# One masked add and one maximum for four heads, and the router's top two moved beside its logits

## The chip, the cores and the metric

One core of a Trainium2 chip runs the whole program in one launch. The metric is the device time in microseconds (us), from launch to end, the median over runs. Everything else of the chip is idle.

## The reference, cut to what matters

x and ctx are 32 batches of 128 rows by 512. One layer of cross attention with 32 heads of 16 columns, then a mixture of 8 experts of which each row takes two.

```python
x = x + xattn(layernorm(x), mask, ctx, Wq, Wk, Wv, Wo, gate)
x = x + moe(layernorm(x), router_w, w1, w2)

# xattn: keys and values of the rows themselves, with a mask, and those of ctx ("adapter"), without
scores = einsum('bhqd,bhkd->bhqk', rope(q), rope(k)) / 4 + mask      # mask is [32, 1, 128, 128]
w = softmax(scores)
attn = w @ v + tanh(gate) * softmax(einsum('bhqd,bhkd->bhqk', rope(q), a_k) / 4) @ a_v
out = attn @ Wo

# moe
logits = x @ router_w.T
topk_vals, topk_idx = top_k(logits, 2)
topk_w = softmax(topk_vals)
# rows sorted by expert, two ragged matmuls with silu(gate) * up between them, weighted and summed
```

## The kernel before, in words

The program has two phases. `attention_phase` (L88) computes attention and the router, batch by batch, and writes for every expert a list of its rows to HBM; `expert_phase` (L1195) walks 71 tiles of 128 list entries. The change touches the first alone.

Each engine has its own instruction stream, written out by hand, and they meet only through semaphores; an `Event` counts one kind of step, and `at(n)` is the count at which batch n has done it. `walk` (L219) gives every engine the same outline: `first`, then one `step` for each batch b, then `last`. Batches 0 to 3 and the last two are written out, the 26 between them run in a loop of 13 iterations of two batches each. A step works on several batches at once: attention proper (exponentials, values) of b; projections, rotation, stacking, scores and maxima of n = b + 1; layer norm of m = b + 2; output projection, second norm and router logits of d = b - 1; the router's choice, counts and lists of c = b - 2.

TensorE's step (L1127) sets the frame. It goes through u = 0 to 15, two for each of eight groups of four heads (own keys and adapter keys). For each u it does `scores_T(b, u)`, which recomputes scores transposed with mask and minus maximum in PSUM, then extra work by u, and `values(b, u - 1)`. The extra work: u = 1 the q projection of n; u = 2 its k projection, `ctx_turn` and `out_turn(d)`; u = 3 `places(c)` (L1121), two small matmuls over the one-hot sum `sel` that count the rows of each expert; u = 4 `out_project(d)`; u = 5 `ak(n)`; u = 7 `h_turn(d)`; u = 8 `router(d)` (its logits go to md[1]); from u = 8 on `stack(n, u - 8)`, and from u = 9 on `scores(n, u - 9)` (L1042). `scores` fills the PSUM banks md[1] (adapter keys) and md[0] (own keys) with a group's scores. Each has a single buffer: the four matmuls into md[1] wait for `s_ad` of the group before, the four into md[0] for `s_own`. After u = 15 come the two value projections and `x_turn(m)`, then `max_turn(n)`.

VectorE's `maxima(n, g)` (L704) reads the two banks: one reduce over md[1] (L707), then for each of four heads a fused instruction that adds the mask to the head's scores in md[0] and keeps the maximum (L710). In the profile each of these is two records, CUSTOM_DVE_ANT_0 and DVE_READ_ACCUMULATOR2_ANT. `neg_max` (L714) turns the maxima of all groups into three bf16 parts; `max_turn` on TensorE and a copy (L731) end the chain, and L731 marks where the next batch's `scores_T` may begin.

The rest of VectorE's step (L855) is in this order: `norm_out(d)`, `sum_out(d)`, `ctx_lo(n)`, `mask_lo(n)`, `out_low(d)`, `rotate_q(n)` (L685, L689), `router_top(c)` (L792), `router_counts(c)`, `rotate_k(n)`, `router_weights(c)`, `values_out(b, 0)`, `residual(d)`, `norm_h(d)`, `h_low(d)`, `ak_low(n)`, `values_out(b, 1)`, `router_logits(d)` (L788), `stats_x(m)`, `maxima(n, 0)`, `norm_x(m)`, `maxima(n, 1)`, `maxima(n, 2)`, `values_out(b, 2)`, maxima 3 to 6, `values_out(b, 3)`, `maxima(n, 7)`, `neg_max(n)`. Here n, m, d and c are left out where there is no such batch: the step of batch 1 has a d and no c.

`router_top` takes the eight logits `lg` of a row, finds the two highest (L796), their gap (L798), and turns each into a one-hot row by way of its lowest index (L802 to L814), then adds the two (`sel`, L818). It is a chain of some 14 instructions over 8 columns, each waiting for the one before. `router_counts` waits for `f_p`, the end of `places`.

GpSimd (POOL) rotates and subtracts for the low halves, and at the end of each step `enter_lists(c)` issues eight indirect DMAs (L425), one for each expert; it does so behind `x_low(m)`, which follows `stats_x` and `norm_x` on VectorE and `x_high(m)` on ScalarE (at u = 11). ScalarE does the exponentials (L528), the copies out of PSUM (`out_T` L543, `stack_out` L513) and the high halves.

Of the kernel before, what the change touches and what calls it, by code (L numbers as in the profile page):

```python
# [21 lines left out]
ALU, ACT, AX = mybir.AluOpType, mybir.ActivationFunctionType, mybir.AxisListType  # L22

P = 128
# [13 lines left out]
GROUPS = NH // 4  # L38
# [49 lines left out]
def attention_phase(nc, ctx, dram, keep):  # L88

    def sb(name, shape, dt):  # L90
        return ctx.enter_context(nc.sbuf_tensor(name, shape, dt))
# [4 lines left out]
    def ev(name, per=1):  # L96
        return Event(keep["semaphores"].enter_context(nc.semaphore(name)), per)
# [23 lines left out]
    msk = sb("msk", [P, 2, P], F32)  # L121
# [17 lines left out]
    mx = sb("mx", [P, 2, NH], F32)  # L139
# [35 lines left out]
    sm = [bank[:, :].rearrange("p (a n) -> p a n", a=4) for bank in md]  # L175
# [22 lines left out]
    w_sc, w_hi, w_lo = ev("w_sc"), ev("w_hi"), ev("w_lo")  # L198

    stk_t, stk_o = ev("stk_t", GROUPS), ev("stk_o", GROUPS)  # L200
    s_pe, s_ad, s_own = ev("s_pe", GROUPS), ev("s_ad", GROUPS), ev("s_own", GROUPS)
    m_part, mp3, mp_t, m_T = ev("m_part", 4), ev("mp3"), ev("mp_t"), ev("m_T")

# [419 lines left out]
    def _(dve):  # L623
# [80 lines left out]
        def maxima(n, g):  # L704
            dve.wait_ge(s_pe.sem, s_pe.at(n, g + 1))
            dve.wait_ge(s_own.sem, s_own.at(n, g))
            dve.tensor_reduce(mx[:, 1, 4 * g:4 * g + 4], sm[1][:, :, :], AX.X, ALU.max).then_inc(s_ad.sem, 1)  # L707
            for j in range(4):
                h = 4 * g + j
                i = dve.tensor_tensor_reduce(sm[0][:, j, :], sm[0][:, j, :], msk[:, n.par, :], 1.0, -3.4028235e38,  # L710
                                             ALU.add, ALU.max, mx[:, 0, h:h + 1])
            i.then_inc(s_own.sem, 1)

        def neg_max(n):  # L714

# [23 lines left out]
        def norm_out(n):  # L739

            dve.wait_ge(av_s.sem, av_s.at(n))
            dve.reciprocal(rc[:, :, :], avs[:, :, :, HD]).then_inc(n_rc.sem, 1)  # L742
            dve.wait_ge(n_rc.sem, n_rc.at(n))
            dve.tensor_tensor(rc[:, :, 1], rc[:, :, 1], tg[:, :], ALU.mult).then_inc(n_rg.sem, 1)
            dve.wait_ge(n_rg.sem, n_rg.at(n))
            dve.tensor_tensor(avs[:, :, 1, 0:HD], avs[:, :, 1, 0:HD],
                              rc[:, :, 1:2].to_broadcast([P, NH, HD]), ALU.mult).then_inc(n_o2.sem, 1)

        def sum_out(n, x_batch):
            if x_batch:  # L750
                dve.wait_ge(x_hi.sem, x_hi.at(x_batch))
                dve.wait_ge(x_lo.sem, x_lo.at(x_batch))
            dve.wait_ge(n_o1.sem, n_o1.at(n))
            dve.wait_ge(n_o2.sem, n_o2.at(n))
            dve.wait_ge(h_hi.sem, h_hi.at(n.shift(-1)))
            dve.wait_ge(h_lo.sem, h_lo.at(n.shift(-1)))
            dve.tensor_tensor(heads(nat), avs[:, :, 0, 0:HD], avs[:, :, 1, 0:HD], ALU.add).then_inc(n_o.sem, 1)
# [30 lines left out]
        def router_logits(n):  # L788
            dve.wait_ge(r_p.sem, r_p.at(n))
            dve.tensor_copy(lg[:, :], md[1][:, 0:NE]).then_inc(r_lg.sem, 1)  # L790
# [64 lines left out]
        def step(b, c, d, n, m):  # L855
            if d:
                norm_out(d)
                sum_out(d, n)
            if n:
                ctx_lo(n)  # L860
                mask_lo(n)
            if d:
                out_low(d)
            if n:
                rotate_q(n)
            if c:
                router_top(c)
                router_counts(c)
            if n:
                rotate_k(n)  # L870
            if c:
                router_weights(c)
            values_out(b, 0)
            if d:
                residual(d)
                norm_h(d)
                h_low(d)
            if n:
                ak_low(n)
            values_out(b, 1)  # L880
            if d:
                router_logits(d)
            if m:
                stats_x(m)
            if n:
                maxima(n, 0)
            if m:
                norm_x(m)
            if n:
                maxima(n, 1)  # L890
                maxima(n, 2)
            values_out(b, 2)
            if n:
                for g in range(3, 7):
                    maxima(n, g)
            values_out(b, 3)
            if n:
                maxima(n, 7)
                neg_max(n)
# [12 lines left out]
        def last(n):  # L912
            norm_out(n)
            sum_out(n, None)
            router_top(n.shift(-1))
            out_low(n)
            router_counts(n.shift(-1))
            router_weights(n.shift(-1))
            residual(n)
            norm_h(n)  # L920
            h_low(n)
            router_logits(n)
            router_top(n)
            router_counts(n)
            router_weights(n)
            experts_slots()

        def experts_slots():
# [37 lines left out]
            assert made[0] == TAB  # L966

        walk(dve, step, first, last)


# [575 lines left out]
```

## Time and profile before

| | us |
|---|---|
| runs | 2768.54, 2767.58, 2760.34; median 2767.58 |
| profiled execution, its own time | 2786.29 |
| its span, first to last instruction | 2784.5 |
| granted clock over the span | 0.830 |
| attention phase, up to the last router work | until about 2283 |
| expert phase | about 501 |
| busy: TensorE, VectorE, ScalarE, GpSimd | 2405.2, 1409.8, 1178.9, 946.0 |

Busy times are sums over the span; a busy TensorE is not a fast one, since the clock it is granted moves between two levels, 1.2 and 2.4 GHz, which the profile shows as 0.50 and 1.00. The line PEclk shows the mean in tenths in 40 slices of 69.6 us, so a slice is about one batch. The chain that ended last is followed back only through the expert phase; for the attention phase waits and timelines must be read. A releaser "remote" means that the wait ended with a semaphore's update that no instruction record explains at that time.

### The profile page before, as it was taken

To read this page: it belongs to the slowest core of one execution; us is meant where nothing else is said; L and a number is where in the kernel's file an instruction comes from. 1 tells how busy PE (TensorE), PEld (TensorE's weight loads), DVE (VectorE), ACT (ScalarE), POOL (GpSimd) and SP (SyncE) were. 2 spreads that over 40 slices of the span, in tenths; PEclk is the share of its full clock that TensorE was granted. 3 is DMA by queue.
4 is the path that set the end of the run, shared out by engine and by line. 5 is a ranking of instruction groups with operands and counts; after the bars stand their busy time and mean duration, and the time that the engine had idled before them with its cause. 6 is when DMAs were issued, how large, how long until landed. Compare 5 with 4: busy or idle time off the path is not lost. (4 is left out here: it accounts for less than half of the span.)

```text
span 2784.5 us, 55409 instructions
## 1 busy us (share of the span) xinstructions
PE 2405.2 (86%) x18441; PEld 1746.0 (63%) x18442; DVE 1409.8 (51%) x4993; ACT 1178.9 (42%) x2100; POOL 946.0 (34%) x948
## 2 busy tenths in 40 slices
PE   4999898889888979898888888888888836999997
PEld 2777666667666756576666666666666624666664
DVE  4466555556555645555555555555555433333332
ACT  3554444444444434344444444444444304444443
POOL 2223333333333333333333333333333223444443
PEclk7898887788788878787878787888788858999999
DMA  2010000000000000010000000000000204444444
GB/s 88 15 38 28 22 23 23 22 23 22 23 22 23 22 13 27 11 32 17 27 16 27 18 25 21 22 23 22 23 22 19 44 14 106 83 83 83 83 83 68
DMA packets 65264, 98.06 MB, mean 35 GB/s; under 512 B 24512, under 2 KB 28608, under 8 KB 64512
## 3 DMA queue, kind: packets, MB, share of 16 engines
q0 software_dynamic: 24096, 37.51, 7.7%
q1 hardware_dynamic: 40928, 57.30, 6.8%
q8 instruction: 156, 2.56, 0.4%
q14 instruction: 84, 0.69, 0.1%
HBM read 59.12 MB, written 35.65 MB: 34 GB/s over the span
## 5 line engine op out<-in xcount | busy, mean ns | idle before, releaser
L1097 PE MATMUL av<-vv,pr 128*128 128x17 f32 x4096 | 636.5, 292 | 6.2 <-ACT pr L528 6.2
L1097 PEld LDWEIGHTS av<-vv,pr 128*128 128x128 f32 x4096 | 628.6, 233 | 20.2 <-ACT pr L528 6.8
L528 ACT ACTIVATE pr<-st 128x512 f32<-128x512 f32 x512 | 305.0, 596 | 587.0 <-PE st L1083 408.6
L707 DVE TENSOR_REDUCE mx<-md 128x4 f32<-128x512 f32 x256 | 176.7, 690 | 340.4 <-remote 214.4
L1051 PE MATMUL md<-kk,qz 128*128 128x128 f16 x2048 | 214.9, 255 | 136.1 <-DVE mx L707 74.7
L1415 PE MATMUL y<-w1s,hgT 128*128 x1704 | 279.2, 314 | 4.4 <-ACT hgT L1329 4.4
L425 POOL DMA_INDIRECT lists<-row,posi x256 | 249.6, 975 | 85.4 <-issue 85.4
L710 DVE CUSTOM_DVE_ANT_0 md<-md,msk 128x128 f32<-128x128 f32 x1024 | 265.0, 321 | 0.0
L1051 PEld LDWEIGHTS md<-kk,qz 128*128 128x128 f16 x2048 | 157.4, 115 | 167.8 <-issue 112.3
L411 POOL TENSOR_TENSOR avs<-avs,rc 128x512 f32<-128x512 f32 x32 | 34.6, 1082 | 662.8 <-DVE rc L742 662.8
L1074 PE MATMUL st<-qz,kk 128*128 128x256 f16 x1024 | 213.8, 293 | 27.8 <-issue 20.1
L520 ACT ACTIVATE qz<-ma 64x256 f16<-64x256 f16 x512 | 191.6, 374 | 104.4 <-remote 86.7
L1083 PE MATMUL st<-mT,hsel 96*128 96x128 bf16 x2048 | 225.7, 238 | 1.1 <-issue 1.1
L1415 PEld LDWEIGHTS y<-w1s,hgT 128*128 128x128 f16 x1704 | 164.2, 98 | 95.8 <-issue 4.9
L737 DVE COPY avs<-av 128x272 f32<-128x272 f32 x128 | 56.5, 441 | 313.9 <-PE av L1097 278.0
L1083 PEld LDWEIGHTS st<-mT,hsel 96*128 96x128 bf16 x2048 | 153.3, 107 | 94.9 <-issue 84.7
L1078 PE MATMUL st<-identr,mskp 128*128 128x512 f32 x512 | 209.5, 495 | 0.0
L522 ACT ACTIVATE kk<-ma 128x512 f16<-128x512 f16 x256 | 152.9, 597 | 3.0
L1434 PE MATMUL y<-w2s,yT 128*128 (+1 forms) x639 | 150.3, 379 | 0.9 <-DVE yT L1393 0.9
L982 PE MATMUL ma<-w_v,xT 128*128 128x512 f16 x384 | 146.5, 559 | 0.0
L710 DVE DVE_READ_ACCUMULATOR2_ANT mx<- 128x1 f32 x1024 | 145.0, 142 | 0.0
L1329 ACT ACTIVATE hgT<-px 128x1024 f16<-128x1024 f16 x71 | 72.7, 1024 | 156.7 <-PE px L1405 156.7
(200 smaller groups left out, 3968.7 us busy)
## 6 DMA issues: line engine op xcount, KB each, us to landing
wst<-in_w SPq DMA_DIRECT2D x32, 352.0 KB, 3.3
cin<-in_ctx SPq DMA_DIRECT2D x32, 256.0 KB, 3.5
xin<-in_x SPq DMA_DIRECT2D x32, 256.0 KB, 3.7
out<-x SPq DMA_DIRECT2D x32, 256.0 KB, 2.0
h_pairs<-ohs SPq DMA_DIRECT2D x32, 256.0 KB
lists<-row,posi POOLq DMA_INDIRECT x256
msk<-in_mask SPq DMA_DIRECT2D x32, 64.0 KB, 3.1
lrow<-lists SPq DMA_DIRECT2D x71, 1.0 KB, 3.6
```

The source lines that it names most:

```text
L425: pool.indirect_dma_start(out=dram["lists"], out_offset=bass.IndirectOffsetOnAxis(ap=posi[:, e:e + 1], axis=0), in_=row[:, e, :], in_offse ...
L520: act.activation(qz[r, pairs, j, :], bank[r, 0:2], ACT.Copy)
L522: act.activation(kk[:, :, pairs, :], keys, ACT.Copy).then_inc(stk_o.sem, 1)
L528: act.activation(pr[:, path, :, :], st[path][:, :, :], ACT.Exp).then_inc(p_ex.sem, 1)
L707: dve.tensor_reduce(mx[:, 1, 4 * g:4 * g + 4], sm[1][:, :, :], AX.X, ALU.max).then_inc(s_ad.sem, 1)
L710: i = dve.tensor_tensor_reduce(sm[0][:, j, :], sm[0][:, j, :], msk[:, n.par, :], 1.0, -3.4028235e38, ALU.add, ALU.max, mx[:, 0, h:h + 1])
L1051: i = pe.matmul(sm[path][:, j, :], qz[:, h // 2, h % 2, :], keys[:, h // 2, :], start=True, stop=True)
L1074: pe.matmul(bank[:, 2 * j:2 * j + 2, :], keys[:, p, :], qz[:, p, :, :], start=(j == 0), stop=False, skip_group_check=True)
L1078: pe.matmul(bank[:, :, :], mskp[:, n.par, part, :], identr[:, :].unsqueeze(1).to_broadcast([P, 4, P]), start=False, stop=False, skip_group ...
L1083: i = pe.matmul(bank[:, j, :], hsel[:, h:h + 1].to_broadcast([3 * NH, P]), mT[:, path, :], start=False, stop=(j == 3), skip_group_check=True)
L1097: i = pe.matmul(av[g // 2 % 2][:, h % 8, path, :], pr[:, path, j, :], vv[:, n.par, path, h, :], start=True, stop=True)
L1415: i = pe.matmul(y1[s.par][j][:, 0:F], hgT[:, s.par, a, c, :], w, start=(n == 0), stop=(n == 11))
```

## The change

In `maxima`, the four fused instructions of a group become one `tensor_tensor` that adds the mask (broadcast over the four heads) to all of md[0] in place, and one `tensor_reduce` over it. A new event `s_mask` makes the reduce wait for the add. `router_top(c)` leaves the head of VectorE's step; `router_top(d)` now stands right behind `router_logits(d)`, one step earlier for the same batch. In `last`, the call for the batch before the last is gone, since its step has done it.

```diff
@@ attention_phase
     stk_t, stk_o = ev("stk_t", GROUPS), ev("stk_o", GROUPS)
+    s_mask = ev("s_mask", GROUPS)
@@ maxima(n, g)
             dve.tensor_reduce(mx[:, 1, 4 * g:4 * g + 4], sm[1][:, :, :], AX.X, ALU.max).then_inc(s_ad.sem, 1)
-            for j in range(4):
-                h = 4 * g + j
-                i = dve.tensor_tensor_reduce(sm[0][:, j, :], sm[0][:, j, :], msk[:, n.par, :], 1.0, -3.4028235e38,
-                                             ALU.add, ALU.max, mx[:, 0, h:h + 1])
-            i.then_inc(s_own.sem, 1)
+            dve.tensor_tensor(sm[0][:, :, :], sm[0][:, :, :], msk[:, n.par, :].unsqueeze(1).to_broadcast([P, 4, P]),
+                              ALU.add).then_inc(s_mask.sem, 1)
+            dve.wait_ge(s_mask.sem, s_mask.at(n, g + 1))
+            dve.tensor_reduce(mx[:, 0, 4 * g:4 * g + 4], sm[0][:, :, :], AX.X, ALU.max).then_inc(s_own.sem, 1)
@@ step(b, c, d, n, m) of VectorE
             if c:
-                router_top(c)
                 router_counts(c)
@@
             if d:
                 router_logits(d)
+                router_top(d)
             if m:
                 stats_x(m)
@@ last(n) of VectorE
             norm_out(n)
             sum_out(n, None)
-            router_top(n.shift(-1))
             out_low(n)
             router_counts(n.shift(-1))
```

## Rows read from the trace of the kernel before

**Rows 1.** The page, part 2: granted TensorE clock in 40 slices of the span.
```profile
PEclk7898887788788878787878787888788858999999
```
**Rows 2.** Windows of whole batches: stretch, length, busy by engine, clock, DMA share, GB/s.
```profile
core 0: us, PE busy (x) PEld busy (x) DVE busy (x) ACT busy (x) POOL busy (x), PEclk, DMA share, GB/s
126.10:177.70 51.60, 49.53 (x470) 37.96 (x470) 31.71 (x110) 30.01 (x57) 14.53 (x11) 1.00 0.09 30
...
1989.60:2061.20 71.60, 61.87 (x472) 46.04 (x472) 39.10 (x137) 30.29 (x58) 22.48 (x20) 0.79 0.07 22
2061.20:2129.60 68.40, 61.39 (x472) 46.00 (x472) 38.95 (x138) 30.57 (x58) 22.49 (x20) 0.80 0.06 19
```
**Rows 3.** Windows within these batches: the stretches at the lower clock.
```profile
2074.60:2081.40 6.80, 6.48 (x25) 3.97 (x26) 4.43 (x19) 1.64 (x3) 2.40 (x2) 0.50 0.00 0
...
2105.30:2125.80 20.50, 18.03 (x96) 14.00 (x97) 8.13 (x42) 5.15 (x12) 4.49 (x5) 0.50 0.01 1
...
2002.90:2013.10 10.20, 7.38 (x32) 4.46 (x31) 7.37 (x24) 4.55 (x7) 4.80 (x3) 0.50 0.00 1
```
**Rows 4.** Waits over the span: total us, times, longest us.
```profile
PE md L1124 <- DVE sel L818: 88.6, 31, 6.0
...
PE md L1051 <- DVE mx L707: 74.7, 52, 4.3
...
PE md L1051 <- DVE mx L710: 20.2, 50, 0.5
```
**Rows 5.** Timeline, VectorE at group 0 and TensorE at group 1.
```profile
2094.84 0.69 DVE L707 TENSOR_REDUCE mx<-md 128x4 f32<-128x512 f32 x1
2095.45 0.29 DVE L710 CUSTOM_DVE_ANT_0 md<-md,msk 128x128 f32<-128x128 f32 x1
...
2096.40 0.54 DVE L650 TENSOR_SCALAR nat<-xin,mv 128x512 f32<-128x512 f32 x1
...
2096.47 0.61 PE L1051 MATMUL md<-kk,qz 128*128 128x128 f16 x8
```
**Rows 6.** Groups of VectorE's instructions: busy us, mean ns, idle before them.
```profile
L710 DVE CUSTOM_DVE_ANT_0 md<-md,msk 128x128 f32<-128x128 f32 x1024 | 265.0, 321 | 0.0
...
L710 DVE DVE_READ_ACCUMULATOR2_ANT mx<- 128x1 f32 x1024 | 145.0, 142 | 0.0
...
L746 DVE TENSOR_TENSOR avs<-avs,rc 128x512 f32<-128x512 f32 x32 | 46.6, 1455 | 1.1
...
L685 DVE TENSOR_TENSOR t<-ma,rope 128x512 f32<-128x512 f32 x64 | 43.8, 685 | 15.5 <-POOL qs L379 14.5 <-PE ma L982 1.0
```
**Rows 7.** Timeline, opening pass: the last of seven such rows, 2.40 us apart.
```profile
62.73 0.69 DVE L707 TENSOR_REDUCE mx<-md 128x4 f32<-128x512 f32 x1 [0.70 <-PE md L1051]
```
**Rows 8.** Timeline of TensorE around `places` in the batch from 2061.2.
```profile
2070.76 1.02 PE L1097 MATMUL av<-vv,pr 128*128 128x17 f32 x8
...
2074.92 0.19 PE L1124 MATMUL md<-sel,tri 128*128 128x8 bf16 x1 [2.69 <-DVE sel L818]
...
2075.01 1.88 PE L1097 MATMUL av<-vv,pr 128*128 128x17 f32 x8
```
**Rows 9.** Groups of TensorE's instructions in the second batch, 126.1 to 177.7.
```profile
L1051 PE MATMUL md<-kk,qz 128*128 128x128 f16 x64 | 5.3, 219 | 1.0 <-DVE mx L710 0.5 <-DVE mx L707 0.4
...
L982 PE MATMUL md<-w_o,oT 128*128 128x512 f16 x12 | 2.8, 380 | 0.7 <-ACT oT L543 0.7
```
**Rows 10.** Timeline of `router_top` in `last`: its first and its last instruction.
```profile
2247.07 0.17 DVE L796 MAX8 top<-lg 128x8 f32<-128x8 f32 x1
...
2249.41 0.17 DVE L818 TENSOR_TENSOR sel<-oh 128x8 bf16<-128x8 f32 x1
```
**Rows 11.** Timeline, second half of the batch from 2061.2, where POOL issues scatters.
```profile
2104.39 0.38 PE L1051 MATMUL md<-kk,qz 128*128 128x128 f16 x4 [0.91 <-DVE mx L707]
...
2111.21 0.69 DVE L707 TENSOR_REDUCE mx<-md 128x4 f32<-128x512 f32 x1 [5.96 <-remote]
```
**Rows 12.** Timeline, L731, where a batch begins; five iterations lie between.
```profile
1429.86 0.29 DVE L731 COPY mT<-md 96x256 bf16<-96x256 bf16 x1 [4.90 <-PE md L1058]
...
2129.60 0.29 DVE L731 COPY mT<-md 96x256 bf16<-96x256 bf16 x1 [4.90 <-PE md L1058]
```

## The prediction

> **What bounds the kernel now.** Read the page first. The clock that TensorE was granted is 0.7 to 0.8 of full in nearly every slice of the batch loop, and 0.9 or more only behind it, in the expert phase [rows 1]. So waits have to be read together with the clock. The table by stretch shows what it is worth: the second batch ran at a clock of 1.00 and took 51.6 us, two late batches with practically the same matmuls (472 against 470) took 71.6 and 68.4 us at 0.79 and 0.80 [rows 2]. Inside the late batches the clock sits at its lower level (1.2 GHz, shown as 0.50) in two places: near the head for 6.8 us (10.2 us in the other batch), and for 20.5 us in the second half [rows 3]. In front of each TensorE had stood idle: 2.69 us for the router's one-hot sum `sel` (L818 to L1124), and in the second half for `maxima` (L707, L710). The list of waits prices these: 88.6 us over 31 batches for `sel`, and 74.7 and 20.2 us for the two halves of `maxima`, 3.1 us a batch [rows 4]. The change touches just these two: it removes the first and makes the chain behind the second longer.
>
> **Maxima, per group.** Before, the first reduce starts at 2094.84, the first fused add-and-maximum at 2095.45 and the next instruction behind the four at 2096.40: 0.61 + 0.95 = 1.56 us, and the signal that frees md[0] comes with the last accumulator read, 1.70 us after the start [rows 5]. The means (321 and 142 ns, four each, 1.85 us) [rows 6] mislead here: read and next instruction overlap, the pitch of a pair is 0.25 us. After, one 128x512 add and one 128x512 reduce stand there. The add in place in PSUM has no row. The nearest is L685, PSUM times a broadcast into SBUF, 685 ns [rows 6]; I take 0.69, and as bounds 0.61, a reduce's pitch, and 1.45, what a contended 128x512 SBUF operation of this kernel (L746) takes [rows 6]. With 0.04 us for the self-wait the group is 0.61 + 0.73 + 0.61 = 1.95 us, **0.39 us longer**, and md[0] is free 2.03 us after the start, 0.33 later. There are fewer records (9 become 3) and more work.
>
> The Trainium skill ("VectorE: DVE Perf Modes", Rules for kernel authors) says the opposite of this part: chained Vector operations always pay for draining, so the instruction count should be cut. With its fixed part of 151 cycles of 0.96 GHz (The TRN2 errata section of the same page), six instructions fewer save 0.94 us and 512 more elements cost 0.53 us: by the rule the group falls from 1.56 to 1.15 us, and the sum below would be some 28 us lower. The 0.25 us pitch above does not bear this out for the fused pair.
>
> Who pays: in the opening pass TensorE and VectorE take turns (VectorE idle 0.70 us before each reduce, seven times) [rows 7], so 8 x 0.33 = **+2.6 us**, once. In a batch the price is inside the stall below. The last maxima and neg_max are covered by the two value projections and cost nothing; without that cover it would be 0.33 us a batch.
>
> **router_top leaves the head.** `sel` is then ready before the batch starts; TensorE's 2.69 us idle ends. With the two small matmuls of places no longer set apart, the value matmuls behind it start 2.9 us earlier than at 2075.01. Eight of them take 1.88 us there and 1.02 us at full clock, just before the gap [rows 8]; if the clock does not fall, the 6.48 us of matmuls in the low stretch [rows 3] take 3.5 us in this proportion: -3.0 us. What is late next: `oT` from ScalarE; the second batch, which has no such gap, waits 0.7 us for it [rows 9], and its clock did not fall. Head: -2.9 - 3.0 + 0.7 = **-5.2 us**. router_counts now waits for `f_p` until TensorE has come to places, with rotate_k, and POOL's rotation behind it, queued; since `f_p` itself comes 2.9 us earlier than before, rotate_k is still earlier than it was and `ak` finds it ready. In every other batch VectorE starts late behind the loop's branch and TensorE idles once more, earlier in the head, so I expect the clock to fall there anyway: the 10.2 us stretch held 7.38 us of matmuls and 2.8 us of idle [rows 3]. The idle goes, some 0.6 us of the matmuls escape the low clock: only -2.8 - 0.3 = **-3.1 us** there.
>
> **router_top arrives in front of maxima(0).** Uncontended it takes 2.4 us (2247.07 to L818 at 2249.41, which the next one overlaps) [rows 10], plus 0.2 us for the wait on `lg`: 2.6 us. At its new place VectorE has no slack: it had waited for values, then it copies lg, does stats_x and begins maxima(0) at 2094.84, while TensorE needs that result at 2096.47 [rows 5]. Queued behind it are stats_x, maxima(0) and norm_x; POOL's and ScalarE's x chain has slack to u = 11. Now: reduce at 2097.5, s_ad at 2098.2, s_own at 2099.55; its last four matmuls follow (half of 0.61 us and the tail), so scores(1) ends at 2100.0 instead of 2097.1: **+2.9 us** of idle, of which 0.33 are the maxima edit.
>
> **What that idle does to the clock.** Less idle was enough before: 0.91 us at 2104.39 [rows 11] and half a microsecond just behind it. So I expect the low stretch to begin at u = 10 or 11, some 7 us of work earlier; it ended only in the dense value projection and will again. At the low clock this mix takes about 1.75 times as long: 1.75 is an estimate, a little under the 1.88 / 1.02 above. From 2097.1 to the old fall at 2105.3 are 8.2 us with 1.4 us idle, 6.8 us of work; less 1.0 before the new fall, x 0.75 = +4.4 us. Against that TensorE is then too slow to wait for maxima: -3.1 us [rows 4]. Net **+1.3 us**. A third thing lies here: while POOL issues its eight list scatters VectorE waits up to 5.96 us for matmuls that had been issued long before ("remote") [rows 11]. POOL starts them behind x_low, so they move along; a slower TensorE should stand less idle in them.
>
> **Sum.** Batches of one kind: -5.2 + 2.9 + 1.3 = -1.0. Of the other: -3.1 + 2.9 + 1.3 = +1.1. A two-batch iteration: +0.1, which is nothing against the errors; five iterations took 699.74 us, 139.95 each [rows 12], so I keep the iteration as it is. What has no counterweight: the second batch has no router work at its head, but gets router_top and the stall. It ran wholly at full clock. There the stall costs 2.9 us, and the work behind it, 5.8 us and the 18.03 us of the long low stretch [rows 3] / 1.75 = 10.3 us, 16 us in all, takes 1.75 times as long, +12: **+15 us**, once. At the end `last` loses a router_top from a chain that nothing covers: **-2.4 us** [rows 10]. Total 2.6 + 15 - 2.4 = +15 us. The profiled execution took 2786.3 us (span 2784.5), 18.7 above the median of the three runs, 2767.6; applied to the median: **2783 us**. A measurement here tells about 0.3% (8 us) from no change.
>
> **Rivals.**
> (a) *The head's gain wins: faster.* It decides where the clock stays up: if the head's low stretch goes in both kinds of batch (the 6.8 us of matmuls that I left at the low clock would take 3.7: another -3.1 us an iteration), and the fall after the stall comes late. For it: both waits at the head get shorter; against it: the earlier idle in every other head stays. 2783 - 14.5 x 3.1 = 2738; with the late fall as well (another -0.7 us an iteration), 2728. Chance 0.25.
> (b) *The records' times add up*, as if nothing overlapped: the group goes from 0.69 + 4 x 0.463 = 2.54 us to 3 x 0.69 = 2.07, so md[0] is free 0.47 us sooner, not 0.33 later. The stall is 0.8 us shorter, 29 x -0.8 = -23, the opening -6: 2754. The means speak for it [rows 6], the starts at a pitch of 0.25 us against it [rows 5]. The Trainium skill's rule above points the same way. Chance 0.08.
> (c) *The in-place add in PSUM is slow*, up to 1.45 us: the stall grows 0.76 us, 29 times: +22; the opening +6: 2811; with an iteration 1.5 us longer as well, 2832. Chance 0.15.
> (d) *An even exchange*: one gap for another, and the second batch's stall is too short to bring its clock down: +3 us, 2770. For it: idle of 0.4 and 0.5 us at the same lines did not bring it down there [rows 9]. Chance 0.12.
> (e) *My forecast*, 2770 to 2798. Chance 0.40, of which 0.05 lie within 0.3%.
> (f) That the change does not do what it says is no case of its own: fewer instructions and a moved call are certain.
>
> So faster 0.25 + 0.08 = 0.33, same 0.12 + 0.05 = 0.17, slower 0.35 + 0.15 = 0.50. The range reaches from (a) to (c): 2728 to 2832.
>
> **What would show it.** Right, if L1124 no longer waits for `sel`, the head of every other batch runs at 1.00, VectorE's reduce of group 0 is late by 2.6 us and L1051 then waits some 2.9 us in every batch from the second on, the low stretch of the second half is near 27 us, VectorE's busy time falls though the pitch of a group grows to 1.95 us, and the second batch takes about 66 us. Wrong, if L1051 does not wait at group 1, if the second batch stays near 52 us, or if the iteration leaves 140 us by more than 1.5 us.

## The result

The changed kernel took 2849.24 us (median of 4, 2836.54 to 2853.30), the kernel before, run beside it, 2768.06: a ratio of 1.0275, interval 1.0243 to 1.0307. It is slower by 81 us of median. The forecast was 2783 with a range up to 2832, so the sign was right and the size was not: most of the loss was in no term of the sum.

### The profile after

The page of the changed kernel, parts 1 and 2:

```profile
span 2844.5 us, 53873 instructions
...
PE 2502.6 (88%) x18441; PEld 1859.4 (65%) x18442; DVE 1453.0 (51%) x3457; ACT 1184.8 (42%) x2100; POOL 943.5 (33%) x948
...
PEclk7977888777778777786888877787778757999999
```

Before, the same line gave TensorE 2405.2 us and VectorE 1409.8 in a span of 2784.5. TensorE has as many matmuls (18441), is busy 97 us longer, and idle 37 us less (341.9 against 379.3). So the 60 us between the two profiled spans are no waiting; they are the same matmuls at a lower clock. The mean granted clock is 0.806, was 0.830. By the starts of L731, 45 of the 60 us lie in the 28 batches from the third to the thirtieth (71.3 us in the mean, 69.7 before), for which the forecast had put nothing, and 16 in the second batch, for which it had put 15.

Windows of batches, as in [rows 2]: the first, second and third, a late one, and inside the second and the late one the stretches at the lower clock.

```profile
core 0: us, PE busy (x) PEld busy (x) DVE busy (x) ACT busy (x) POOL busy (x), PEclk, DMA share, GB/s
73.90:122.30 48.40, 46.06 (x430) 35.56 (x430) 25.02 (x49) 26.98 (x53) 11.02 (x8) 1.00 0.07 21
...
122.30:190.10 67.80, 63.80 (x470) 49.74 (x470) 36.26 (x76) 30.55 (x57) 14.50 (x11) 0.77 0.07 23
190.10:264.70 74.60, 64.44 (x472) 49.59 (x472) 39.03 (x90) 30.63 (x58) 22.66 (x20) 0.75 0.07 21
1975.80:2048.00 72.20, 66.64 (x472) 52.42 (x472) 40.55 (x90) 30.84 (x58) 22.45 (x20) 0.74 0.07 22
2002.00:2022.50 20.50, 20.50 (x145) 18.47 (x145) 10.76 (x31) 10.16 (x21) 4.63 (x6) 0.50 0.18 57
2025.90:2043.00 17.10, 15.62 (x91) 13.28 (x92) 8.45 (x14) 5.13 (x11) 2.50 (x3) 0.50 0.01 1
155.40:186.10 30.70, 30.16 (x182) 25.80 (x182) 16.05 (x29) 10.15 (x21) 1.15 (x1) 0.50 0.00 1
```

The second batch did what was forecast for it (about 66 us; 67.8, from 51.6). The late batch did not: it has no low clock at its head any more, but two long low stretches, 37.6 us in all, against 27.3 and 30.7 in the two late batches of [rows 2, 3]. The first of them starts 26 us into the batch, which here is counted from L731. What stands there is in the list of waits (total us, times, longest us):

```profile
PE md L975 <- DVE ohs L786: 41.1, 28, 4.6
PE md L1050 <- DVE mx L708: 30.7, 40, 3.0
PE md L1050 <- DVE mx L712: 45.7, 75, 0.9
PE md L981 <- ACT oT L544: 20.7, 31, 1.1
PE md L1123 <- DVE sel L818: 3.0, 1, 3.0
DVE pos L823 <- PE md L1124: 101.9, 31, 5.1
DVE t L686 <- POOL qs L380: 47.7, 29, 5.2
```

The wait for `sel` is gone (88.6 before, [rows 4]) and `oT` is what is late next, both as forecast. New is the first line: `h_turn` (L975, L976 before) waits for `ohs`, the normalised residual in halves. Before, that was 6.0 us in the whole run. The two lines of `mx` do not hold all of TensorE's waiting at the second group: in eight batches its first part, 1.6 us, stands in the list under `kk` (28.3 us in 14 waits in all). Where it comes from is in VectorE's timeline of the late batch (start, length, in brackets the idle before):

```profile
1986.87 0.17 DVE L823 TENSOR_TENSOR pos<-md,count 128x8 f32<-128x8 f32 x1 [2.84 <-PE md L1124]
...
1988.83 0.69 DVE L686 TENSOR_TENSOR t<-ma,rope 128x512 f32<-128x512 f32 x1 [1.59 <-POOL qs L380]
...
1992.83 2.10 DVE L849 CAST posi<-pos 128x8 int32<-128x8 f32 x1
...
1995.24 0.44 DVE L737 COPY avs<-av 128x272 f32<-128x272 f32 x1 [0.20 <-DVE tok L852]
1995.59 0.68 DVE L767 SCALAR_TENSOR_TENSOR x<-md,xres 128x512 f32<-128x512 f32 x1
...
2000.06 0.69 DVE L786 TENSOR_TENSOR ohs<-nat,ohs 128x512 f16<-128x512 f32 x1 [0.69 <-ACT ohs L550]
```

and TensorE's:

```profile
2000.81 0.62 PE L975 MATMUL md<-ident,ohs 128*128 128x128 f16 x8 [1.87 <-DVE ohs L786]
```

VectorE now stands idle in `router_counts` and in `rotate_k`, `router_weights` ends in a conversion of eight numbers that takes 2.10 us (0.17 in the batch of [rows 5] before), and when the queue comes to the values and the residual (L767) they are overdue. Before, the same place had a reserve. This row of the kernel before was not read for the forecast:

```profile
2083.50 0.44 DVE L737 COPY avs<-av 128x272 f32<-128x272 f32 x1 [3.73 <-PE av L1097]
```

VectorE had waited 3.73 us for TensorE there. The shorter head of TensorE used that up, and 1.87 us more: TensorE comes to `h_turn` 23.1 us into this batch and starts it at 25.0; in the batch of that row it did both at 28.2.

### The profile page after: what moved, and what is told of

Its sections match the earlier page's. It is cut to its first block and busy times, and to the rows that moved or that the text cites. A ratio compares the mean times of both kernels' runs of the same rounds, so it can differ in the third digit from the quotient of the medians.

```text
span 2844.5 us, 53873 instructions
## 1 busy us (share of the span) xinstructions
PE 2502.6 (88%) x18441; PEld 1859.4 (65%) x18442; DVE 1453.0 (51%) x3457; ACT 1184.8 (42%) x2100; POOL 943.5 (33%) x948
## 5 line engine op out<-in xcount | busy, mean ns | idle before, releaser
L1096 PEld LDWEIGHTS av<-vv,pr 128*128 128x128 f32 x4096 | 673.1, 247 | 25.2 <-ACT pr L529 11.8
L1096 PE MATMUL av<-vv,pr 128*128 128x17 f32 x4096 | 677.0, 302 | 11.1 <-ACT pr L529 11.1
L1050 PE MATMUL md<-kk,qz 128*128 128x128 f16 x2048 | 252.0, 282 | 128.7 <-DVE mx L712 45.7
L708 DVE TENSOR_REDUCE mx<-md 128x4 f32<-128x512 f32 x256 | 176.7, 690 | 296.5 <-remote 155.3
L1050 PEld LDWEIGHTS md<-kk,qz 128*128 128x128 f16 x2048 | 189.1, 131 | 163.7 <-issue 67.9
L1073 PE MATMUL st<-qz,kk 128*128 128x256 f16 x1024 | 228.1, 310 | 28.6 <-issue 21.0
L1082 PE MATMUL st<-mT,hsel 96*128 96x128 bf16 x2048 | 243.3, 252 | 0.0
L1077 PE MATMUL st<-identr,mskp 128*128 128x512 f32 x512 | 223.8, 525 | 0.0
L712 DVE TENSOR_REDUCE mx<-md 128x4 f32<-128x512 f32 x256 | 177.1, 692 | 8.7
L709 DVE TENSOR_TENSOR md<-md,msk 128x512 f32<-128x512 f32 x256 | 176.5, 690 | 0.0
L1073 PEld LDWEIGHTS st<-qz,kk 128*128 128x128 f16 x1024 | 118.9, 151 | 33.0 <-issue 22.4
```

Of the source, the lines that this page charges most:

```text
L712: dve.tensor_reduce(mx[:, 0, 4 * g:4 * g + 4], sm[0][:, :, :], AX.X, ALU.max).then_inc(s_own.sem, 1)
L1050: i = pe.matmul(sm[path][:, j, :], qz[:, h // 2, h % 2, :], keys[:, h // 2, :], start=True, stop=True)
L1073: pe.matmul(bank[:, 2 * j:2 * j + 2, :], keys[:, p, :], qz[:, p, :, :], start=(j == 0), stop=False, skip_group_check=True)
L1077: pe.matmul(bank[:, :, :], mskp[:, n.par, part, :], identr[:, :].unsqueeze(1).to_broadcast([P, 4, P]), start=False, stop=False, skip_group ...
L1082: i = pe.matmul(bank[:, j, :], hsel[:, h:h + 1].to_broadcast([3 * NH, P]), mT[:, path, :], start=False, stop=(j == 3), skip_group_check=True)
L1096: i = pe.matmul(av[g // 2 % 2][:, h % 8, path, :], pr[:, path, j, :], vv[:, n.par, path, h, :], start=True, stop=True)
```

## The experiments

Each kernel is the kernel before with the edits named. Ratios are to the kernel before on the same chip. TensorE's busy time and the clock are those of the profiled execution. A point is 0.01 of the ratio.

```
edits                                          ratio    interval          TensorE  clock
new maxima (N)                                 0.9905   0.9862 to 0.9947  2342.9   0.859
router_top behind router_logits (L)            1.0419   1.0358 to 1.0480  2506.2   0.803
N + L: the change                              1.0275   1.0243 to 1.0307  2502.6   0.806
router_top in neg_max's wait (S)               1.0306   1.0263 to 1.0349  2485.6   0.808
N + S                                          1.0007   0.9972 to 1.0042  2449.2   0.823
router_weights behind h_low (W)                1.0044   1.0025 to 1.0062  2380.0   0.844
N + L + W                                      0.9968   0.9929 to 1.0006  2429.4   0.833
S + W                                          0.9580   0.9545 to 0.9614  2309.3   0.864
N + S + W                                      0.9472   0.9436 to 0.9508  2315.4   0.871
N + S + W, router_counts behind rotate_k       0.9630   0.9588 to 0.9673  2312.9   0.872
N + S + W, dummy ahead of the residual         1.0404   1.0342 to 1.0466  2542.0   0.794
N + S + W, dummy ahead of maxima(1)            0.9748   0.9714 to 0.9783  2323.6   0.871
N + S + W, dummy in L's place                  0.9991   0.9960 to 1.0023  2431.4   0.832
one more maximum in each group (old form)      1.0115   1.0089 to 1.0142  2372.7   0.841
scatters ahead of stage_a                      1.1043   1.0995 to 1.1092  2638.0   0.768
N + scatters ahead of stage_a                  1.1095   1.1041 to 1.1149  2638.2   0.769
```

### Which half of the change costs

The new maxima alone:

```diff
-            for j in range(4):
-                h = 4 * g + j
-                i = dve.tensor_tensor_reduce(...)
-            i.then_inc(s_own.sem, 1)
+            dve.tensor_tensor(sm[0][:, :, :], ...).then_inc(s_mask.sem, 1)
+            dve.wait_ge(s_mask.sem, s_mask.at(n, g + 1))
+            dve.tensor_reduce(mx[:, 0, 4 * g:4 * g + 4], ...).then_inc(s_own.sem, 1)
```

> Only the maxima are changed (one mask addition and one maximum for four heads); router_top stays at the head of the iteration. Theory M (the new maxima are the loss): 2830 to 2850 us. Theory P (the loss is router_top's new place, by a wait at the second group of scores and by a late head of VectorE): the opening pass grows by 8 x 0.33 = 2.6 us, and each of the 31 batches by at most 0.39 us beyond that, so 2770 to 2785 us; h_turn waits for VectorE as briefly as before (6 us in all), and the stall of TensorE at the second group stays under 0.5 us a batch.

It gave 0.9905: against both numbers, the maxima alone make the kernel faster. router_top's move alone:

```diff
-                router_top(c)
                 router_counts(c)
...
                 router_logits(d)
+                router_top(d)
```

> Only router_top is moved behind router_logits; the four fused mask-and-maximum instructions of a group stay. Theory P: most of the loss is here, 2825 to 2850 us; h_turn's wait for ohs is some 1.3 us a batch (40 us in all, 6 before) and the scores of the second group wait some 2.4 us more. Theory M: 2760 to 2775 us, as before.

It gave 1.0419 (2885 us), more than the whole change. The loss is the move; with it, the new maxima give 1.4 points back. `h_turn` waits 44.9 us here.

### Which of the two waits that the move leaves

```diff
-        def neg_max(n):
+        def neg_max(n, d=None):
...
+            if d:
+                router_top(d)
```

In this kernel router_top stands inside neg_max, behind the copy of the partial maxima, and not behind router_logits.

> Fused maxima kept; router_top(d) is put behind the copy of the partial maxima inside neg_max, where VectorE waits about 4.9 us for TensorE's transpose, so it delays no maximum of scores. Theory T (the wait at the second group of scores is the loss): that wait is gone and the time falls to 2750 to 2775 us. Theory H (the head is the loss: with router_top gone from it TensorE runs ahead, and VectorE's router_weights, stretched beside GpSimd, comes late for the residual that h_turn needs): h_turn's wait of some 1.3 us a batch stays and the time stays at 2790 to 2830 us.

It gave 1.0306 (2860 us), above the 2830 us that were expected at most: with the old maxima the wait at the second group of scores was worth about 1.1 points, and most of the loss stayed, with `h_turn`'s wait at 48.8 us. Then router_weights was put behind the residual as well:

```diff
             if n:
                 rotate_k(n)
-            if c:
-                router_weights(c)
             values_out(b, 0)
...
                 h_low(d)
+            if c:
+                router_weights(c)
```

> As the kernel with router_top in neg_max's wait, and router_weights(c) is moved from behind rotate_k to behind h_low(d), so VectorE has the residual's input ahead of h_turn as early as it can. Theory H: h_turn's wait is back to under 10 us in all, the wait for sel stays gone, and the time falls below the kernel before: 2690 to 2745 us. Theory T: no change against the kernel with the slot alone (within 10 us), since the head is not what costs.

It gave 0.958 (2660 us), 200 us below the kernel with S alone, and below the lower end that was expected. `h_turn`'s wait is back to 6.0 us in 2 places, TensorE is busy 176 us less. The same edit on the changed kernel, and on the kernel before:

> The changed kernel with one more edit: router_weights(c) behind h_low(d) and not behind rotate_k, so the residual is not behind it. Theory H (the loss is h_turn's wait for VectorE at 25 us of a batch and the slow clock that follows it): the wait of 41 us in all goes to under 8 us, the low clock starts at the second group of scores and not at h_turn, and the time falls by 140 to 190 us, to 2660 to 2710 us. Theory T (the wait at the second group of scores costs most): 2820 to 2850 us.

> The kernel before with router_weights(c) alone moved behind h_low(d); router_top stays at the head, so TensorE still waits 2.7 to 2.9 us for sel. Theory H: before, VectorE waited 3.7 us for values(3) ahead of the residual, so router_weights cost nothing there, and its move alone gives 2745 to 2775 us. If the move were good by itself, whatever the head does: 2660 to 2700 us.

The first gave 0.9968 (2776 us): 3.1 points better than the change, but only half of what was expected. The second gave 1.0044 (2799 us), 24 us above the 2775 expected at most: the move by itself gains nothing, so router_weights costs nothing in its old place as long as TensorE's head is long. That it loses 0.4 points shows as waiting: TensorE is busy 25 us less and idle 40 us more. With router_top in neg_max's wait and the new maxima, but router_weights in its old place:

> The changed kernel with router_top moved from behind router_logits into neg_max's wait; router_weights stays where it was. Theory H and T together (each of the two waits alone is enough to bring the low clock on, so taking one away gives little): 2810 to 2845 us, against 2849 of the changed kernel. Theory T alone: 2740 to 2790 us.

It gave 1.0007 (2781 us), better than the 2810 us at least that was expected. So taking away one of the two waits gives 2.7 or 3.1 points, and both together, with the new maxima in all of these,

> New maxima, router_top in neg_max's wait, router_weights behind h_low. If the effects of the parts add up as ratios (maxima 0.9905, the other two 0.958): 2625 to 2650 us. If the maxima's gain was a chance of how the clock fell in that kernel: 2655 to 2700 us.

give 0.9472 (2631 us), 8.0 points less than the change, where the two single steps add up to 5.8. It beats both kernels. One more edit on it, router_counts behind rotate_k:

> The kernel with all three edits (new maxima, router_top in neg_max's wait, router_weights behind h_low), and router_counts(c) behind rotate_k(n), not in front of it, so rotate_k no longer waits 2.8 us behind the counts' wait for TensorE. If VectorE's head is still what GpSimd and TensorE wait for: 2590 to 2622 us. If it is covered: 2622 to 2640 us, as without this edit (2631).

gave 0.963, slower than without it and above both ranges that were expected. Its list of waits names the place: out_project (L984), which in the kernel without this edit never waits for router_counts (L827), now does.

```profile
PE md L984 <- DVE count L827: 39.0, 25, 2.0
```

TensorE's busy time is the same and its idle time 45 us longer. No run took this wait away by itself.

### The waits by themselves

The edits above move work as well as waits. So each wait was put back into the fastest kernel with one dummy instruction. First ahead of the residual:

```diff
             if d:
+                dve.tensor_reduce(pad[:, 0:17], ident16[:, :].unsqueeze(1).to_broadcast([P, 17, P]), AX.X, ALU.max)
                 residual(d)
```

> The fastest kernel so far (all three edits, 2631 us) with one more VectorE instruction ahead of the residual, a maximum over 17 x 128 numbers of a constant tile that nothing reads, some 2.3 us long (an estimate from 0.61 us for 512 numbers). It leaves no work out. Theory H (the wait at h_turn and the slow clock behind it cost some 5 us a batch): h_turn waits 1.9 us again, the low clock starts at 26 us of a batch and not at 40, and the time is 2760 to 2800 us, as in the kernel with router_top in neg_max's wait and router_weights in its old place (2781). If a wait costs only its length: 31 x 1.9 = 59 us, so 2680 to 2700 us. If the old place of router_weights costs by something else (its stretched instructions): 2631 to 2660 us.

It gave 1.0404, 9.8% above the kernel without the dummy, more than any reading expected. A wait of it, its total, and two windows, a batch and the stretch right behind the wait:

```profile
1145.04 0.62 PE L980 MATMUL md<-ident,ohs 128*128 128x128 f16 x8 [1.86 <-DVE ohs L789]
```

```profile
PE md L980 <- DVE ohs L789: 64.0, 32, 4.6
```

```profile
1120.00:1192.30 72.30, 66.87 (x472) 52.50 (x472) 39.87 (x90) 30.83 (x57) 22.49 (x20) 0.74 0.07 22
1146.60:1167.10 20.50, 20.40 (x145) 18.38 (x143) 9.46 (x22) 10.29 (x22) 4.84 (x6) 0.50 0.15 49
```

The fastest kernel has 6.0 us in that line of waits and 2315.4 us of TensorE. The dummy adds 58 us of wait, and the two profiled spans differ by 240 us (2866.2 and 2626.0), 227 of them TensorE's busy time. The batch is the changed kernel's late batch again: low from 26 us on, 145 matmuls in 20.5 us, in both. For comparison a batch of the fastest kernel and its one low stretch:

```profile
1003.00:1066.80 63.80, 57.48 (x472) 44.13 (x472) 37.34 (x89) 31.46 (x58) 22.48 (x20) 0.87 0.08 25
1043.40:1060.50 17.10, 15.74 (x91) 13.28 (x92) 6.24 (x10) 5.14 (x11) 3.84 (x4) 0.50 0.02 1
```

So a wait of 1.9 us in the dense part of the batch costs 7.7 us a batch. In 28 of the 30 batches with the wait the low clock starts 26 to 29 us into the batch; without it, in 29 of 30 at 39 us or later. That `h_turn`'s wait causes the early fall, and the fall a loss, is shown. Its size depends on the kernel around it: with router_weights in its old place (N + S) the wait is 34.5 us longer in all than in the fastest kernel and the profiled span 153 us longer, 4.4 times as much, where the dummy has 4.1; in the changed kernel, where the other wait is there as well, taking it away gave only 3.1 points.

Then a dummy ahead of the second group's maxima (between maxima(0) and maxima(1)):

> The fastest kernel so far with one more VectorE instruction ahead of the maxima of the second group, over 16 x 128 numbers, some 2.1 us long, in router_top's new place or nearly so. It leaves no work out. Theory H and T (the wait at the second group brings the slow clock on at 33 us of a batch): 2750 to 2790 us, as in the changed kernel with router_weights moved (2776). If a wait costs only its length: 31 x 1.1 to 1.6 = 34 to 50 us, so 2665 to 2685 us.

It gave 0.9748, 2.8 points above the kernel without it. The sum of the waits does not show what it did: TensorE stood 54.7 us for L709's maxima, against 52.6 without the dummy. The timeline does, here in the batch from 1415.1:

```profile
1449.50 0.38 PE L1056 MATMUL md<-kk,qz 128*128 128x128 f16 x4 [1.30 <-DVE mx L709]
1450.74 0.40 PE L1056 MATMUL md<-kk,qz 128*128 128x128 f16 x4 [0.86 <-DVE mx L713]
```

The dummy delays the second group's maxima, so TensorE waits at the third group of scores and not at the second, 34 us into the batch. The fastest kernel has a pair of the same length (1.33 and 0.86 us), but at 39.5 us: the wait was moved forward, not added. The low clock then starts at 36 to 38 us in most batches. So this kernel does not reproduce the wait of the change, but it shows that the place of a wait counts and not its length alone. The same dummy exactly where router_top stands in the change, ahead of stats_x:

```diff
                 router_logits(d)
+                dve.tensor_reduce(pad[:, 0:16], ident16[:, :].unsqueeze(1).to_broadcast([P, 16, P]), AX.X, ALU.max)
```

> The fastest kernel so far (0.947 of the kernel before) with one dummy maximum of VectorE over 16 x 128 numbers (2.28 us) in router_top's new place, right behind router_logits and ahead of stats_x. It leaves no work out. If the place costs by the delay alone, in whatever way: TensorE waits 1.3 to 1.6 us for the maxima at 32 to 34 us of a batch, the low clock starts there, and the ratio is 0.985 to 1.005, as in the changed kernel with router_weights moved (0.997). If only the length of the wait counts, or if the rest of that kernel's loss lies in something else: 0.955 to 0.98.

It gave 0.9991, where the changed kernel with router_weights moved has 0.9968: a delay of 2.3 us of VectorE in that place explains router_top's price there. (The list of waits of that changed kernel puts 56.2 us of TensorE under `kk`, and this one's only 3.8. The wait so named in its batch from 1427.7 ends 0.15 us behind the end of the first reduce. So does the first wait shown below, and that one ends before the `kk` under way is ready. So the name is most likely wrong, and it is the same wait for the maxima.) Its timeline and windows:

```profile
1109.41 0.38 PE L1055 MATMUL md<-kk,qz 128*128 128x128 f16 x4 [1.23 <-DVE mx L709]
1110.65 0.40 PE L1055 MATMUL md<-kk,qz 128*128 128x128 f16 x4 [0.86 <-DVE mx L713]
```

```profile
1077.40:1146.20 68.80, 63.68 (x472) 49.28 (x472) 39.74 (x91) 30.41 (x58) 22.46 (x20) 0.78 0.07 23
1111.00:1141.70 30.70, 29.07 (x176) 24.69 (x176) 15.30 (x27) 9.82 (x21) 9.07 (x10) 0.50 0.01 1
```

The low clock starts 34 us into the batch, and not 40, and lasts 30.7 us and not 17.1. In order of place, then, over the fastest kernel: 9.3 points for a wait of 1.9 us at 25 us, 5.2 for one of 1.2 + 0.9 us at 32 us, 2.8 for one of 1.3 + 0.9 us at 34 us.

### Why the new maxima gain

The kernel before was given a longer group without the new form: one maximum of 2 x 128 numbers of the mask ahead of the four fused pairs.

> The kernel before with one more VectorE instruction in each group, a maximum over 2 x 128 numbers of the mask that nothing reads, which lengthens the group's maxima by some 0.35 us as the new form does (1.94 against 1.56). It leaves no work out. Theory C (the new maxima gain because a longer group spaces TensorE's work so that the clock falls later or for less): 2735 to 2760 us, as with the new maxima alone. Theory I (the gain comes from the smaller number of instructions): 2775 to 2800 us.

It gave 1.0115 (2814 us), above both ranges: the longer group does not gain, it costs. The two kernels differ in one place above all, the long wait of the maxima while GpSimd issues its eight list scatters [rows 11]. One such wait of each, the new form first, then the padded one:

```profile
1471.33 0.69 DVE L708 TENSOR_REDUCE mx<-md 128x4 f32<-128x512 f32 x1 [3.44 <-remote]
```

```profile
1566.68 0.69 DVE L708 TENSOR_REDUCE mx<-md 128x4 f32<-128x512 f32 x1 [6.35 <-remote]
```

The scatters had begun at 1462.76 and 1555.07, so the reduce starts 8.6 and 11.6 us behind the first; before it was 10.1. In the median batch it is 8.6, 11.6 and 10.1. The times of the three kernels stand in the same order (0.9905, 1.0115, 1). The next two kernels move the scatters, with the old and with the new maxima:

```diff
+            if c:
+                enter_lists(c)
             if m:
                 stage_a(m)
                 x_low(m)
-            if c:
-                enter_lists(c)
```

> The kernel before, with GpSimd's eight scatters of a batch issued ahead of stage_a and x_low instead of behind them, some 12 us earlier, where TensorE works on the gates and the first scores. Theory S (a group's maxima start 10.1 us after the first scatter, whatever TensorE has done, since its semaphore updates come late while the scatters are issued): the maxima's wait of 5.9 us is gone from its place (214 us in all falls under 120, or turns up as waits of other lines), and the time changes by more than 0.5% in one direction or the other. Theory N (the wait has another cause, such as TensorE's own order): the wait stays where it is, and the time stays within 0.5% unless the later stage_a costs something.

> The kernel with the new maxima alone, with the scatters moved as in the run with the earlier scatters. Theory S: the new maxima gained 1% only because the late update fell 1.2 us earlier (median 8.9 us behind the first scatter, 10.1 before, 11.6 in the padded kernel), so against the kernel with the earlier scatters and the old maxima this one is no faster: 0 to 25 us slower. Theory I (fewer instructions gain in themselves): it is 15 to 35 us faster than that one.

They gave 1.1043 and 1.1095. From the waits and the timeline of the first:

```profile
DVE avs L737 <- remote: 229.6, 28, 8.4
...
DVE mx L707 <- remote: 17.2, 3, 8.0
```

```profile
1164.52 0.95 POOL L425 DMA_INDIRECT lists<-row,posi  x1 [0.30 <-issue]
...
1167.18 0.44 DVE L737 COPY avs<-av 128x272 f32<-128x272 f32 x1 [8.32 <-remote]
```

The late updates went with the scatters: the maxima's 214.4 us before fell to 17.2, and the copy of the values (17.9 us before) now waits 229.6. There, with the phase of the scatters changed, the new maxima no longer gain (9 us slower by the medians, within the two intervals). That fits the reading that their 1% came only from where the late update fell; it does not exclude that something of the new form helps in its old surroundings. What the new maxima give differs from kernel to kernel: 1.0 point alone, 1.4 with L, 3.0 with S, 1.1 with S + W. Only the first was looked into; that the gain is 3.0 with S stays open. The 10% of both kernels are not resolved into their parts: GpSimd's stage for the next batch is later too.

## Why the prediction was wrong

**Maxima, per group: right.** In the late batch the group's starts are

```profile
2010.86 0.69 DVE L708 TENSOR_REDUCE mx<-md 128x4 f32<-128x512 f32 x1
2011.47 0.69 DVE L709 TENSOR_TENSOR md<-md,msk 128x512 f32<-128x512 f32 x1
2012.19 0.69 DVE L712 TENSOR_REDUCE mx<-md 128x4 f32<-128x512 f32 x1
2012.80 0.54 DVE L651 TENSOR_SCALAR nat<-xin,mv 128x512 f32<-128x512 f32 x1
```

0.61 + 0.72 + 0.61 = 1.94 us; 1.95 was worked out. The add in place in PSUM takes 690 ns, as its nearest row said, and rival (c), a slow add, is out. In the opening pass, [rows 7], two of seven rows:

```profile
63.48 0.69 DVE L708 TENSOR_REDUCE mx<-md 128x4 f32<-128x512 f32 x1 [0.70 <-PE md L1050]
...
66.20 0.69 DVE L708 TENSOR_REDUCE mx<-md 128x4 f32<-128x512 f32 x1 [0.70 <-PE md L1050]
```

2.73 us apart by the mean of the six steps, from 2.40: +0.33 a group, as taken, and the first batch starts 3.0 us later for +2.6 forecast. Rival (b) is refuted by these starts: six instructions fewer took 0.38 us more. The 1.15 us that were worked out from the rule of the Trainium skill ("VectorE: DVE Perf Modes", Rules for kernel authors) fail with it for this group. The prediction said that VectorE's busy time would fall; it rose, from 1409.8 to 1453.0 us (to 1488.2 with the maxima alone; router_top's move by itself lowers it to 1377.2). The records of the old form overlap (its 265.0 and 145.0 us in [rows 6] are partly the same time), the new ones hardly, and the forecast's own 1.95 against 1.56 should have said so.

**router_top leaves the head: right in what it priced, wrong in what it left out.** The wait for `sel` went, `oT` costs 20.7 us in 31 waits (0.7 each, as taken), and the head runs at full clock in nearly all batches, of both kinds. Up to `h_turn` the gain came in: TensorE is there at 23.1 us of the batch, 28.1 before, for the -5.2 of the sum. In the other kind of batch it is there at about 24.3 us, 31.2 before: some 7 us, and not 3.1, since the low clock went there too.

The failed step is that the head's term ends there: it has a price for `oT` and finds `ak` ready, and puts the wait of `h_turn` for VectorE at nothing, without naming it. What the prediction says of rotate_k is true, it starts 13.0 us into the late batch and not 14.3. But it followed one chain behind router_counts and not the other: rotate_k, router_weights, values, residual, norm_h, h_low, `h_turn`. TensorE's way there had become 5 us shorter, VectorE's had not, and the reserve was 3.73 us. In addition VectorE came, later in its queue, under GpSimd's subtractions with other instructions than before: L849 from 231 to 1750 ns in the mean, while L808, which had carried that delay before at 1898 ns, stands now at 167. That extra time of L849, 1.9 us, is as long as the wait in the late batch. From the fifth to the thirtieth batch `h_turn` waits 0.8 to 2.0 us in 23 of 26, and in 18 of them the low clock starts at 26 to 27 us. With the wait out (N + L + W) the changed kernel stands at 0.9968 and not at 1.0275: the missing term is 3.1 points, some 85 us, where the forecast missed by 66.

**router_top in front of maxima(0): right where it can be seen alone, in the second batch.** TensorE waits at the second group

```profile
154.05 0.38 PE L1050 MATMUL md<-kk,qz 128*128 128x128 f16 x4 [1.44 <-DVE mx L708]
155.30 0.56 PE L1050 MATMUL md<-kk,qz 128*128 128x128 f16 x4 [0.86 <-DVE mx L712]
```

2.30 us for the 2.9 of the sum, the low stretch from there is 30.7 us (27 forecast), and the batch is 16.2 us longer (+15 forecast). In the late batch above the wait is not there at all: the clock had fallen at `h_turn` and TensorE was too slow to have to wait. In eight of the later batches it had not fallen, and there the wait is as in the second (1.6 us, under `kk`, and 0.86). So the claim "L1051 then waits some 2.9 us in every batch" is wrong where the clock has fallen already.

**The clock term: near what was measured.** The sum gave +1.3 us a batch to the earlier fall, with 1.75 as its estimate of the slowing. With the other wait absent the measured price of this place is 5.0 to 5.2 points (0.9968 and 0.9991 against 0.9472), some 140 us or 4.5 us a batch, waits included; 2.9 + 1.3 = 4.2 was near that. The head's gain against it, -5.2 and -3.1, was mostly lost again at `h_turn`. The changed kernel without that wait, 0.9968, lies 0.9 points below the forecast's 1.0056, so the other terms do not add up exactly either: prices of waits do not, as the last section shows.

**`last`: wrong.** From its start to the end of the span went 591.4 us before (2193.15 to 2784.5) and 593.1 after (2251.44 to 2844.5). The -2.4 us did not come. Up to the last wait for `sel` the two traces give, before and after:

```profile
2193.15:2267.00 73.85, 48.10 (x325) 38.09 (x326) 26.75 (x98) 17.17 (x29) 20.91 (x23) 0.69 0.26 44
```

```profile
2251.44:2326.00 74.56, 55.00 (x324) 43.12 (x324) 24.87 (x85) 17.16 (x29) 20.83 (x23) 0.61 0.26 44
```

TensorE's wait of 6.04 us for `sel`, 56.5 us behind that start, is gone, but the same matmuls take 6.9 us longer at a lower clock. The prediction gave this stretch no clock term. That the one caused the other was not tested.

**The rivals.** (d), the even exchange, is out by the second batch, whose clock did fall. (a) was right in its condition, that the head's low stretch goes in both kinds of batch, and wrong in the time, since the clock fell early at `h_turn`. With both waits gone the head's gain does win, by 5.3% (new maxima and router_weights' new place included) and not by 1%: that rival priced the head's clock, and not what a batch is worth in which nothing brings the clock down before 39 us. The forecast's range did not hold the result because no rival had a second wait in it. The sign was right by the smaller part of the loss: the sum's +15 us are the second batch and the opening, and these came in (16.2 and 3.0 us). The 45 us of the later batches were in no term, and that they have the same sign is luck.

## What to carry to other kernels

When a change takes a wait out of one engine's stretch, all of that engine's next meetings with the others move earlier: list each of them with the idle time that the other engine had there, and compare that reserve with what is saved. Where the clock follows the waits, read a wait by where it stands: one of 1.9 us in dense work cost 7.7 us a batch here, four times itself, and one that was only moved from 39.5 to 34 us of a batch cost 2.8 points. The cure was then cheap: work that nobody waits for soon (the router's weights) behind work that TensorE waits for, and a chain of small operations in a wait that exists anyway.

## What the hardware showed that was not expected

- The price of a wait is not additive. With the new maxima in all four kernels, the ratio is 1.0275 with both waits (at `h_turn` and at the second group), 0.9968 and 1.0007 with one, 0.9472 with none: once either has brought the lower of the two clock levels (1.2 GHz for 2.4), the other finds TensorE slow already.
- Two operations of VectorE on 8 columns took 2.0 to 2.15 us in place of 0.17 when they fell under GpSimd's 128x1024 subtraction (2.12 us), and which of them stood there changed with the edit: L808 before (29 of 32, mean of all 1898 ns), L849 after (26 of 32, 1750 ns); with router_weights moved L849 is back at 171 ns.
- While GpSimd issues its eight indirect DMAs, 1.27 us apart, work that waits on TensorE starts late, by up to 8.4 us at the values' copy, and this moves with them: 214.4 us at the maxima before, 229.6 us at the values' copy with the scatters earlier. That it is the update of the semaphore that is late is how the profile's "remote" is read here; no run showed the delivery itself.
